# Two further fp32 products of constants behind each part of a one-core graph kernel's last product

## What is computed

```python
h = batch_norm(x)
a_in  = segment_sum((h @ W_in  + b_in )[src] * iw[:, None], dst)
a_out = segment_sum((h @ W_out + b_out)[dst] * ow[:, None], src)
h = gated_update(concat(a_in, a_out), h)
x = layernorm(x + h)
f = (x - mean(x, 0)) / (std(x, 0) + 1e-4)
y = segment_sum(edge_weight[:, None] * f[src], dst) @ weight + bias
x = layernorm(x + y)
```

## Time and profile before

| | value |
|---|---|
| median of three runs | 3501.4 us |
| span of the profiled execution | 3959.9 us |
| PE busy | 2627.5 us, 66% |
| DVE busy | 2300.7 us, 58% |
| POOL busy | 2609.5 us, 66% |
| indirect DMAs issued by POOL | 3 lines of 832 |
| mean granted TensorE clock | 0.819 |
| DMA | 565.23 MB, mean 143 GB/s |

### The profile page before, as it was taken

How to read it: one execution, slowest core, us unless ns; L and a number is a source line. 1 busy time by engine, 2 the same in 40 slices (tenths; PEclk the granted TensorE clock), 3 DMA queues, 4 the chain that set the end, 5 groups by cost and what they waited for, 6 DMA issues and landing times.

```text
span 3959.9 us, 46668 instructions
## 1 busy us (share of the span) xinstructions
PE 2627.5 (66%) x10701; PEld 1902.7 (48%) x10701; DVE 2300.7 (58%) x4513; ACT 1060.1 (27%) x3135; POOL 2609.5 (66%) x2706
## 2 busy tenths in 40 slices
PE   4665665666566665558888888996645655555477
PEld 4454543333343333337777777643434433434355
DVE  6866875656565565646666666686334444444355
ACT  3243322222222222234444444462000000000012
POOL 5666666666666666666666666477667777677764
PEclk7777888777787777779999999998777767677689
DMA  5443343333343333347888888654333333333333
GB/s 148 138 132 105 95 138 134 133 132 133 130 137 131 129 135 134 129 153 243 246 247 246 246 246 247 184 164 138 91 91 93 94 93 91 91 93 93 93 117 97
DMA packets 275049, 565.23 MB, mean 143 GB/s; under 512 B 55599, under 2 KB 121126, under 8 KB 274787
## 3 DMA queue, kind: packets, MB, share of 16 engines
q0 software_dynamic: 119808, 329.02, 26.7%
q1 hardware_dynamic: 146452, 223.99, 18.6%
q10 hardware_dynamic: 8528, 9.30, 0.7%
HBM read 419.19 MB, written 142.88 MB: 142 GB/s over the span
## 4 chain that ended last, share of the span: by engine, by line
PE 36%; another core or an unknown queue 25%; DVE 16%; issue 12%; POOL 5%; ACT 3%; DMA 2%; DVEq 1%; SPq 0%; ACTq 0%; POOLq 0%
PE ps L1145 10%; PE ps L958 9%; PE ps L1215 7%; PE ps L1078 3%; POOL arena L549 3%; DVE arena L2162 2%; ACT arena L735 2%; POOL messages L555 2%; DVE arena L1781 2%; PE ps L1106 2%; PE ps L1178 2%; DVE arena L1762 1%; DVE node_a L2176 1%; DVE arena L2168 1%
## 5 line engine op out<-in xcount | busy, mean ns | idle before, releaser
L555 POOL DMA_INDIRECT messages<-arena x832 | 830.4, 998 | 418.5 <-issue 243.2
L549 POOL DMA_INDIRECT arena<-in_x,arena x832 | 791.6, 951 | 468.4 <-issue 205.9
L625 POOL DMA_INDIRECT arena<-x_table,wh x832 | 844.0, 1014 | 358.7 <-issue 240.4
L1215 PE MATMUL ps<-arena 128*128 x2048 | 596.1, 448 | 407.1 <-issue 214.1
L1215 PEld LDWEIGHTS ps<-arena 128*128 128x128 f32 x2048 | 449.3, 226 | 557.6 <-issue 489.5
L958 PE MATMUL ps<-arena 128*128 128x128 f32 x3328 | 489.6, 309 | 248.6 <-issue 178.0
L958 PEld LDWEIGHTS ps<-arena 128*128 128x128 f32 x3328 | 459.7, 220 | 332.0 <-issue 282.5
L735 ACT ACTIVATE arena<-ps,arena 128x256 f32<-128x256 f32 x832 | 325.2, 481 | 901.1 <-remote 498.8
L1078 PE MATMUL ps<-arena 128*128 128x256 f32 x1664 | 489.3, 447 | 9.6 <-issue 5.3
L2176 DVE TENSOR_TENSOR node_a<-node_a,ps 128x256 f32 x256 | 106.8, 417 | 642.8 <-remote 482.2
L1078 PEld LDWEIGHTS ps<-arena 128*128 128x128 f32 x1664 | 379.2, 230 | 97.1 <-issue 32.9
(11 more groups left out here) (283 smaller groups left out, 3462.9 us busy)
## 6 DMA issues: line engine op xcount, KB each, us to landing
arena<-messages SPq DMA_DIRECT2D x464, 260.0 KB
arena<-in_x SPq DMA_DIRECT2D x304, 128.0 KB, 2.9
gate_rows<-arena SPq DMA_DIRECT2D x49, 384.0 KB
arena<-gate_rows SPq DMA_DIRECT2D x49, 384.0 KB, 3.0
arena<-in_x,arena POOLq DMA_INDIRECT x832
messages<-arena POOLq DMA_INDIRECT x832
arena<-x_table,wh POOLq DMA_INDIRECT x832
arena<-in_x SPq DMA_DIRECT2D x48, 256.0 KB
```

The costliest lines, as they stand in the source:

```text
L549: nc.gpsimd.indirect_dma_start(out=big[:, s, j, 0:D], out_offset=None, in_=x, in_offset=bass.IndirectOffsetOnAxis(ap=ids[:, j:j + 1], axis ...
L555: nc.gpsimd.indirect_dma_start(out=messages, out_offset=bass.IndirectOffsetOnAxis(ap=ids[:, j:j + 1], axis=0), in_=big[:, s, j, :], in_off ...
L625: nc.gpsimd.indirect_dma_start(out=last_rows[:, (g + 1) % LAST_ROWS, j * D:(j + 1) * D], out_offset=None, in_=x1_table, in_offset=bass.Ind ...
L1215: last = nc.tensor.matmul(ps[g % LAST_SUMS][:, 0:D], last_hot[h][:, j, :], last_rows[:, bass.ds(k, 1), j * D:(j + 1) * D].rearrange("p o d ...
```

## The change

Behind each part with number up to 207, that is behind 208 parts, TensorE makes two products of constants into PSUM bank 5: the stationary operand is `ident` (128x128), the moving operand is `iota`, its 128 columns read four times over (512 columns), both fp32. Nothing waits for them, nothing reads them, and they raise no semaphore. They stand behind `second_mm` of their part and ahead of the callback's work.

```diff
+            def keep_busy(to, n):
+
+                for _ in range(n):
+                    nc.tensor.matmul(to[:, :], ident[:, :], iota[:, :].rearrange("p (o n) -> p o n", o=1).broadcast_to([P, 4, P]),
+                                     start=True, stop=True)
+
...
                     last.then_inc(S["second_mm"], 1)
+                    if g <= FIRST_END:
+                        keep_busy(ps[5], 2)
                     if after:
                         after(i, s)
```

## The result

The changed kernel takes 3521.32 us (median of six runs, 3513.44 to 3527.92), the kernel before 3501.72 us (six runs, 3501.19 to 3512.27). The ratio is 1.0051, with a 95% interval of 1.0037 to 1.0065: slower by 13 to 23 us. Measured again beside the kernel before, it was 1.0053 (1.0039 to 1.0067). The forecast was no change.

The account below looks back on a forecast made before the run. GpSimd's chain of indirect DMAs was taken as the bound, with hardly a wait in ordinary runs. Cost 0 and gain 0 gave 3501.4 + 0 - 0 = 3501.4 us, range 3488 to 3545 us.

Parts of the forecast that it names:

- What bounds the kernel: Whole kernel: an ordinary run is a chain of GpSimd's DMAs in three loops with hardly a wait, plus gates of 220 us.
- the sum: Whole kernel: profiled span 3959.9 us less 455.7 us of GpSimd's waits gives 3504.2 us, against a median of 3501.4 us.
- the 0.70 us steps: TensorE, last stage: gaps of 0.70 and 1.40 us between instructions, taken for an effect of the profiler's recording.
- The price of the additions on TensorE: Last stage: two products take 1.72 us at full clock, 357.8 us over 208 parts; TensorE's share becomes 82%.
- the ring's reserve: GpSimd's row buffers, last stage: a part may be some 30 us late before GpSimd has to wait.
- the first rival: TensorE, last stage: clock stays at 0.75, 94 us slower, likelier 10 to 40 us; decided at 0.85; chance 0.13.
- cost 0: Last stage: at full clock no part exceeds GpSimd's pace of 4.27 us, so the additions add no time.
- What they are added to: TensorE, last stage: demand of 894 us in 1094 us, below GpSimd's pace except in the first 24 parts, 1 us behind.
- The queue behind them: Work behind the additions: VectorE's add does not wait, sums of squares come up to 1.72 us later, off the path.
- the second: TensorE, last stage: 0.70 us gaps also occur in ordinary runs, 5.6 us per part hit; some 30 us slower; chance 0.07.
- the third: Last stage: GpSimd does wait in ordinary runs, so full clock wins up to 27 us, likelier 3490 us; chance 0.08.
- both slower rivals: Last stage: clock does not follow, or the 0.70 us gaps are real in ordinary runs; chance of slower 0.20.

Follow-up runs that it names:

- the undisturbed profile: The kernel before, unchanged, profiled once more: 3505.91 us (a single run), span 3504.1 us.
- two ahead: Changed kernel with its two products put ahead of each part instead of behind it: 3515.79 us, 1.0038 of the kernel before.
- a later VectorE: Changed kernel, additions moved to bank 4, with one VectorE copy into PSUM bank 5 ahead of the one-hot operations: 3503.51 us, 1.0006 of the kernel before.

## Why the prediction was wrong

**What bounds the kernel** was right. In an ordinary run GpSimd issues its DMAs without a wait in the last product; 3504.2 us from the sum, 3504.1 us in the span of the undisturbed profile. That the two agree to 0.1 us is luck: the idle time before the three loops' DMAs is 431.9 us shorter there, not 455.7, and some waits remain in the first two loops. The reading of the 0.70 us steps as something that ordinary runs do not have was right as well, as far as these profiles go: the second one lacks them. What makes them was not tried.

**The price of the additions on TensorE** was right. A product takes 0.86 us at full clock, the demand stays below GpSimd's pace, the ring's reserve of some 30 us holds, and the clock rose to 0.98, well past the 0.85 on which the first rival hung. With three and four products the runs met sums made of the same terms within 11 us.

**The step that failed** is the term "cost 0" under *What they are added to* and *The queue behind them*. It took the 844.0 us of GpSimd's DMAs as fixed and asked only whether GpSimd would wait. The text followed what VectorE waits for (not the additions) but not when VectorE runs. The rows had the hint: DMAs of the same size from 943 to 1492 ns, and a mean of 1014 ns in the last product against 951 ns for the first gathers. On the engine that is the bound, a spread of durations is a cost with a cause, and what moves the cause moves the time. In place of 0, the step cost 15.8 us of busy time in one profile of the changed kernel and 14.8 us in the other, on DMAs that start while a one-hot operation with both inputs in SBUF runs.

**The rivals.** The clock followed, so the first did not come. The 0.70 us steps were not in these runs, so the second did not. GpSimd did not wait in the kernel before, so there was nothing for the third to win. The forecast of "slower" had the right sign in both slower rivals and the wrong mechanism. The 3521.3 us lie inside the stated range, which had been stretched for these rivals; that is luck and not a merit of the working.

**Open.** Why this change moves the starts to a worse place is not shown. A guess: with the clock at 0.98, parts that wait for their rows end at a more regular distance from a DMA's start, and the one-hot operations behind them with it. The DMA time is 839.9, 842.2, 855.7 and 841.5 us for none, one, two and three products, 850.1 us with two ahead and 838.8 us with two and a later VectorE. The counts of DMAs that start 0.04 to 0.30 us behind the begin of a one-hot operation go nearly in the same order: 88, 93, 133, 96, 108 and 82. That says where the time is lost, but nothing here gives these counts ahead of a run, and no run separates the clock from the delay.

## What to carry to other kernels

Where GpSimd issues indirect DMAs back to back and is the bound, compare their durations with the shortest one: what is above it is time of the kernel, and here it came from VectorE operations with two operands in SBUF that were running when a DMA started. Give such operations one operand in PSUM before tuning anything else; the form with the numbers in PSUM and a scalar per partition took 29 us off here, while a fuller TensorE took nothing off, since GpSimd did not wait for it. A change on an engine that is not on the path can still cost if it moves in time what the bound engine collides with.

## What was not expected of the hardware

- A DMA of GpSimd is held up only if its start falls inside the VectorE operation, by what is left of it less some 0.13 us: at 3205.16 us, 0.34 us left, 1.16 us in place of 0.95 us. In the kernel before, 233 of the 234 DMAs of L625 that start 0.06 us or more behind the begin of a large operation with two SBUF operands follow this within 0.03 us. If the operation starts 0.10 us after the DMA, it costs nothing.
- The edge is sharp, and it works the other way too. Of the 27 DMAs of the changed kernel that start in the first 0.04 us of a one-hot operation one is held up; the others take their usual time. The operation is the one that takes longer then: 0.74 us on average, against 0.69 us.
- The same work of VectorE with the compared operand in PSUM (1.36 us for each part) cost the DMAs nothing.
- Two profiles of one unchanged program had spans of 3959.9 and 3504.1 us, and register operations of TensorE's sequencer of up to 707 and 71 ns. A profile whose span is far from the time of the runs is a reason to subtract its waits, as was done here, or to take another.
